# First cross attention: VectorE copies half of the last turned keys and takes the first maxima as keys arrive; the first scales of the last feed-forward are loaded in the SSM layer

## The reference, cut to what matters

```python
q, k, v = _fq_sym(q * scale, -1), _fq_sym(k, -1), _fq_sym(v, 2)   # round(x/s) clipped to +-127, times s
attn = softmax(einsum('bhqd,bhkd->bhqk', q, k))
attn = _fq_unsigned(attn, -1)                                      # s = row maximum / 255
x = x + einsum('bhqk,bhkd->bhqd', attn, v).reshape(B, N, C) @ Wp + bp
```

```python
vals = NVFP4_LUT[idx].reshape(N, K // 32, 32) * scales[:, :, None]    # gate, up, down
out = einsum('tn,hn->th', gelu_tanh(x @ Wg.T) * (x @ Wu.T), Wd)
```

## Time and profile before

| | us |
|---|---|
| median of three runs | 1578.74 |
| profiled execution, its own time | 1576.28 |
| its span | 1574.6 |
| TensorE busy | 1397.5 (89%) |
| VectorE busy | 1095.3 (70%) |
| ScalarE busy | 865.7 (55%) |
| GpSimd busy | 444.6 (28%) |
| mean granted clock of TensorE | 0.935 |

### The profile page before, as it was taken

The page is one execution under the profiler, slowest core; times in us unless marked ns, Lnnn a source line. Parts: engine busy times, 40 slices in busy tenths (PEclk is TensorE's granted clock), DMA queues, the critical chain, the costliest instruction groups (busy, mean ns, idle before and its releaser), DMA issues. The chain is left out here.

```text
span 1574.6 us, 23902 instructions
## 1 busy us (share of the span) xinstructions
PE 1397.5 (89%) x8036; PEld 981.6 (62%) x8036; DVE 1095.3 (70%) x2239; ACT 865.7 (55%) x2299; POOL 444.6 (28%) x515
## 2 busy tenths in 40 slices
PE   7876989866999689998679899999998989999969
PEld 5653444434776347876557678787877446666657
DVE  4687989834666566664568776765663779999953
ACT  2446989842123355425444545545454579999831
POOL 2244000000000000530346325533500047777710
PEclk9986999977999789998789999999999999999979
DMA  4001999975340322300200000000002344433120
GB/s 147 1 1 41 180 182 186 185 176 166 112 162 0 78 63 41 109 1 1 68 14 14 14 14 2 14 1 1 1 1 69 101 146 121 117 102 104 41 80 8
DMA packets 192390, 112.89 MB, mean 72 GB/s; under 512 B 150233, under 2 KB 166617, under 8 KB 191628
## 3 DMA queue, kind: packets, MB, share of 16 engines
q1 hardware_dynamic: 192268, 111.35, 27.6%
HBM read 77.51 MB, written 0.26 MB: 49 GB/s over the span
## 5 line engine op out<-in xcount | busy, mean ns | idle before, releaser
L671 DVE TENSOR_REDUCE x_row_max<-banks 128x1 f32<-128x512 f32 x248 | 152.6, 682 | 14.3 <-PE banks L365 13.9
L574 ACT ACTIVATE x_v_full<-banks,x_neg_max,x_q_scale 128x1024 int16<-128x1024 f32 x128 | 153.3, 1202 | 14.8 <-DMA x_v_full<-x_v_full 7.8
L211 PE MATMUL banks<-a_w_ring,x_normed_T 128*128 128x512 f32 x320 | 148.0, 603 | 4.8 <-DVE a_r L3189 4.8
L2670 DVE TENSOR_TENSOR ctx_tokens<-ctx_tokens,banks 128x512 f32<-128x512 f32 x128 | 87.8, 686 | 82.1 <-ACT x_weights_T L2556 60.2
L2388 PE MATMUL banks<-ctx_tokens,x_kT 128*128 128x512 f32 x272 | 140.1, 602 | 2.9 <-ACT ctx_tokens L2550 2.3
L2409 PEld LDWEIGHTS banks<-x_v,x_weights_T 128*128 128x128 f32 x896 | 113.0, 194 | 20.8 <-issue 17.6
L2409 PE MATMUL banks<-x_v,x_weights_T 128*128 128x129 f32 x896 | 118.1, 278 | 2.1 <-ACT x_weights_T L2566 2.1
L365 PE MATMUL banks<-x_kT_parts,x_qT_int 64*128 64x512 bf16 x512 | 105.2, 409 | 7.0 <-DVE x_row_max L671 3.3
L2504 POOL TENSOR_TENSOR ctx_tokens<-ctx_tokens 128x512 f32<-128x512 f32 (+1 forms) x48 | 65.8, 1372 | 141.7 <-DVE ctx_tokens L2650 141.7
L426 PEld LDWEIGHTS banks<-x_v_full,x_v_int 128*16 128x16 f16 x1024 | 57.5, 91 | 75.8 <-DMA x_v_full<-x_v_full 41.9
L211 PEld LDWEIGHTS banks<-a_w_ring,x_normed_T 128*128 128x128 f32 x320 | 59.6, 194 | 69.4 <-issue 69.4
(11 more groups left out here) (527 smaller groups left out, 3240.8 us busy)
## 6 DMA issues: line engine op xcount, KB each, us to landing
a_w_ring<-in_L_attn_WB_T SPq DMA_DIRECT2D x16, 512.0 KB
a_w_ring<-in_L_attn_WC_T SPq DMA_DIRECT2D x16, 512.0 KB
f_w_gate_up<-in_L_ffn_gate_up SPq DMA_DIRECT2D x18, 352.0 KB
ctx_tokens<-in_ctx SPq DMA_DIRECT2D x16, 256.0 KB, 5.8
x_wq<-in_L_xattn_Wq_T SPq DMA_DIRECT2D x8, 512.0 KB, 3.7
a_w_ring<-in_L_attn_Wth_T SPq DMA_DIRECT2D x8, 512.0 KB
a_bias_ring<-in_L_attn_B_bias_perm SPq DMA_DIRECT2D x16, 256.0 KB
a_bias_ring<-in_L_attn_C_bias_perm SPq DMA_DIRECT2D x16, 256.0 KB
```

The lines of the kernel that those rows point to most:

```text
L211: last = nc.tensor.matmul(out, lhsT, rhs, start=(i == 0), stop=(i == len(pairs) - 1))
L574: nc.scalar.activation(eb[:, q % RING], k.ps[:, 2 + 2 * (q % 2):4 + 2 * (q % 2), :].rearrange("p a n -> p (a n)"), ACT.Exp, bias=nb[:, v % ...
L671: nc.vector.reduce_max(mx[:, u % 2, i:i + 1], k.bank(MBANK[m % 3]), AX.X).then_inc(s.max_taken, 1)
L2670: nc.vector.tensor_tensor(flat(top), flat(top), bank, ALU.max).then_inc(s.maxed, 1)
```

## The change

In the first cross attention, for the last three pairs of keys (`ALONE` = 13 and up), ScalarE copies only the first block of a pair and VectorE the second, with a semaphore of its own, `kT_half_taken`. `kt_taken` is the wait for either. The maxima of tiles 4 to 7 move between these copies, on TensorE and on VectorE. GpSimd's casts of the values move one round later. ScalarE's wait for the cleared `ot` moves to its first write there.

In the other part a tile `first_scales` is allocated outside the layers. Its three loads are issued in the SSM layer, behind w_out; the feed-forward loads chunks 1 to 3 only and reads chunk 0 from the new tile.

```diff
+        ALONE = NP - 3
+        def kt_taken(engine, j, i):
+            if j < ALONE:
+                engine.wait_ge(s.kT_taken, 2 * j + i + 1)
+            elif i == 0:
+                engine.wait_ge(s.kT_taken, 2 * ALONE + j - ALONE + 1)
+            else:
+                engine.wait_ge(s.kT_half_taken, j - ALONE + 1)
...
                         if j >= 1:
-                            pe.wait_ge(s.kT_taken, 2 * (j - 1) + i + 1)
+                            kt_taken(pe, j - 1, i)
...
-                for i in range(4, 8):
-                    first_max(i)
+                    if j == NP:
+                        first_max(4)
+                        first_max(5)
+                    if j > NP:
+                        first_max(5 + j - NP)
...
-                    if NP // 2 + 4 <= j < NP // 2 + 8:
-                        g = j - NP // 2 - 4
+                    if NP // 2 + 5 <= j < NP // 2 + 9:
+                        g = j - NP // 2 - 5
...
                 def take_keys(j):
-                    for i in range(2):
+                    for i in range(1 if j >= ALONE else 2):
...
                 def take_output(v):
+                    if v == 0:
+                        act.wait_ge(s.zeroed, 2)
...
                 act.wait_ge(s.v_ready, 4)
-                act.wait_ge(s.zeroed, 2)
...
+                def take_half(j):
+                    dve.wait_ge(s.kT_in_psum, 2 * j + 2)
+                    a = (2 * j + 1) * P
+                    nc.vector.tensor_copy(kt[:, :, a:a + P], k.ps[:, 5, :].bitcast(BF16).rearrange("p (h n) -> p h n", n=P)).then_inc(s.kT_half_taken, 1)
+                for j in range(NP, NP + 3):
+                    take_half(j - 3)
+                    if j == NP:
+                        first_max(4)
+                        first_max(5)
+                    else:
+                        first_max(5 + j - NP)
```

```diff
@@ l3_attn, SyncE, behind the load of w_out
+                for j in range(len(MATS)):
+                    sp.dma_start(k.first_scales[:, j], A["L3_ffn_scales_T"][j, :, 0:CW].unsqueeze(1).to_broadcast([8, 16, CW])).then_inc(k.p_loaded[0], 16)
@@ l3_ffn
-                for c in range(NC):
+                for c in range(1, NC):
...
+                    by = k.first_scales[:, j] if c == 0 else scale[:, j, sl]
@@ build
+        k.first_scales = k.sb("f3_first_scales", [P, len(MATS), CW])
```

More of the change, by code:

```diff
@@ L273, in l0_xattn @@
         names = ("dve_step ctx_first x_loaded wq_loaded filled masks_ready bias_loaded bias_ready3 k_in_psum v_in_psum k_taken v_taken kf_ready hi_ready mid_ready "
[L274 removed]
+                 "rest_ready parts_ready kT_in_psum kT_taken kT_half_taken q_in_psum q_parts_ready qT_in_psum qT_taken xt_ready vmax_ready vmaxT_in_psum "
                  "vdiag_ready vscale_in_psum vscale_ready v_int_ready v_ready max_scores max_taken bias_ready exp_scores exp_done pT_used "
@@ L368, in first_max @@
                 def first_max(i):
-                    pe.wait_ge(s.kT_taken, 4 * (i + 1))
+                    for half in range(2):
+                        kt_taken(pe, 2 * i + 1, half)
                     if i >= 2:
@@ L506, in _ @@
                         nc.gpsimd.tensor_tensor(part(m, 2), kr[:, m % 2], part(m, 1), ALU.subtract).then_inc(s.parts_ready, 1)
-                    if NP // 2 + 4 <= j < NP // 2 + 8:
-                        g = j - NP // 2 - 4
+                    if NP // 2 + 5 <= j < NP // 2 + 9:
+                        g = j - NP // 2 - 5
                         pool.wait_ge(s.v_int_ready, g + 1)
                         nc.gpsimd.tensor_copy(vq[:, VG * g:VG * (g + 1)], vi[:, g]).then_inc(s.v_ready, 1)
-                pool.wait_ge(s.kT_taken, NKT)
+                kt_taken(pool, NP - 1, 0)
+                kt_taken(pool, NP - 1, 1)
                 nc.gpsimd.memset(ot[:], 0.0).then_inc(s.zeroed, 1)
@@ L3315, in weights @@
                     sl = slice(c * CW, (c + 1) * CW)
+                    by = k.first_scales[:, j] if c == 0 else scale[:, j, sl]
                     value = k.fp4[:, j, sl].bitcast(F8).rearrange("p (n v) -> p v n", v=2)
-                    nc.vector.scalar_tensor_tensor(out=wd[:, j, c % 2], in0=value, scalar=64.0, in1=scale[:, j, sl].unsqueeze(1).to_broadcast([P, 2, CW]),
+                    nc.vector.scalar_tensor_tensor(out=wd[:, j, c % 2], in0=value, scalar=64.0, in1=by.unsqueeze(1).to_broadcast([P, 2, CW]),
                                                    op0=ALU.mult, op1=ALU.mult).then_inc(s.w_ready, 1)
```

1 line of the change is left out of this document (removed).

## The result

| | before | after |
|---|---|---|
| median, us | 1578.74 (1577.45 to 1583.26, 5 runs) | 1565.41 (1563.71 to 1572.09, 5 runs) |
| profiled execution, its own time | 1576.28 | 1565.09 |
| its span | 1574.6 | 1563.3 |
| mean granted clock | 0.935 | 0.938 |

The changed kernel is faster: ratio 0.9918, 95% interval 0.9901 to 0.9936. A second measurement of the changed kernel (e14) gave 0.9930 (0.9916 to 0.9944).

A forecast was written before the change was run, and what follows sets the result against it. Bounds: waits for scales in the last feed-forward and for the memset and last keys in the first cross attention. Gains of 2.3 and 2.7 us, together 5.0, off 1578.74 gave 1573.7 us; range 1570.2 to 1577.3.

The forecast's parts named there:

- T2: Last feed-forward, scales loaded early: first product 4.67 us earlier, less 2.0 for a clock fall, 2.7 us gained.
- Rival 1: Last feed-forward: the clock holds through TensorE's gap, early scales give 4.7 us, total 1571.7 us; chance 0.25.
- T1: First cross attention: earlier memset release, shared key copies and moved casts together gain 2.3 us.
- T1b: First cross attention, last keys: VectorE takes three copies from ScalarE; 0.3 us gained, or 0.2 lost if copies are slow.
- T1a: First cross attention: ScalarE no longer waits for GpSimd's memset before its table load; 1.3 us gained.
- T1c: First cross attention: GpSimd's casts one round later no longer slow VectorE's product of keys; 0.7 us gained, bound 0.
- Rival 2: First attention gives nothing, as transposing DMAs bind the stage behind the exponentials; 1576.0 us; chance 0.15.
- rival 3: Last feed-forward: second scale group lands no earlier, first product stays, only the attention gain remains; 1576.4 us; chance 0.08.
- rival 4: Stage of exponentials: ScalarE runs ahead, waits for transposing DMAs grow, kernel slower, up to 1586.6 us; chance 0.06.

The follow-up runs named there:

- e14: Changed kernel itself, unchanged, measured a second time against the kernel before: ratio 0.9930 (0.9916 to 0.9944).
- e2: Kernel before with only the scales part (`first_scales`) of the change added: ratio 0.9951.
- e4: Kernel before itself, unchanged, measured and profiled once more: ratio 0.9991.
- e10: Kernel before with two more VectorE maximum operations behind the last addition of the first cross attention: second feed-forward 77.03 us.
- e11: Kernel before with one more VectorE maximum operation behind the last addition of the first cross attention: third self-attention 46.40 us.
- e16: Kernel before with one small VectorE maximum more, its result unread, behind the first cross attention: median 1574.70 us, ratio 0.9975.
- e17: Kernel before with one VectorE memset split in two in the third feed-forward, behind the layers in question: second feed-forward 79.62 us.
- e3: Kernel before with only ScalarE's wait for the cleared output tile moved to its first output: ratio 0.9988.
- e6: Changed kernel without the scales part and with GpSimd's casts in their old rounds: ratio 0.9967.
- e15: Kernel before with GpSimd's memset of the output tile split into two halves: 5 us slower (2 to 7).
- e8: Changed kernel with the second chunk's scales loaded behind the third's: last feed-forward 61.22 us.

## Why the prediction was wrong, point by point

Two steps failed: a fall of the clock that did not come, and the layers outside the diff, which the sum put at nothing. Of the 8.3 us between forecast and median, 2.0 stand against the first and some 3 against the second. Earlier loads are 0.75 us, the attention 0.2 to 0.5, and 2 us are left.

**T2, the clock's price: the first step that failed.** The forecast took 4.67 us of earlier product and subtracted 2.0 for a fall of the clock in a gap of 2.4 us. The product came 5.4 us earlier against its norm (11.10 instead of 16.52 us behind it): 4.67 and 0.75 for loads that landed sooner. That they landed sooner because nine stood in the queue and not twelve is not shown: in e2, also with nine, the same three landed 8.47 us behind the first issue, as the first three did before, and with twelve the first three landed anywhere from 7.6 to 8.6 us behind it. And the clock did not fall. T2 was 5.4 in place of 2.7, also alone (e2: 4.7). I had interpolated a threshold between a gap of 1.24 us that held and one of 2.9 that fell. The runs show gaps of 1.94, 2.05 and 2.72 that held and one of 2.09 that fell. The gap's length alone does not decide in that stretch, so from the rows of before neither outcome could be called the likelier. Rival 1 had 0.25 and came nearest, with 1571.7.

**T1, the attention: about right.** In x0 seven profiled kernels with the copies took 331.3 to 333.9 us, mean 332.4. Seven with neither the copies nor any edit of the waits (before, e2, e4, e10, e11, e16, e17), less what their added operations take, took 333.2 to 338.1, mean 335.2. That is 2.8 us for 2.3 forecast, with a scatter of 1 to 2 us between executions. Counted from the key product of round 13 to the first exponential, where most of the scatter is gone, it is 2.5 us (32.9 instead of 35.4 in the mean of the same kernels), and from there to the next layer both groups take the same (196.4 and 196.5 us, again less the added operations), as the forecast assumed. The parts were differently mixed. T1b was the largest, 1.7 us from e3 to e6: the copy takes 0.69 us, and TensorE turned the last pair at the higher clock. T1a was smaller, 0.8 us in e3, since the table load is now late for TensorE's scores. T1c was 0.2 to 0.3 us beside the copies: the small operation that waits beside the cast (1.65 us) takes back most of what the product gains. That is near its bound 0. That VectorE's copies do not wait for the casts beside them is borne out: the copies at 136.29 and 138.74 lie in the casts of 135.10 and 138.05 and take 0.69 us all the same.

**The untouched layers: the second step that failed.** The sum T1 + T2 puts every other layer at nothing and gives no reason for it. 2.5 us in f1 or a2 and some 0.5 in x2, f2 and x3 came with every kernel that has VectorE instructions added ahead of them, be it one or three. By their ratios e16, e10 and e11, less the operations' own 0.4, 2.5 and 1.2 us, give 4.3, 3.4 and 2.1 us; I take 3. The profile of before does not show which side of the clock's step a layer will come to lie on, so the size could not be forecast. But the layers behind the change have low-clock stretches, and the range had no room for such a step.

**The sum.** 5.4 + 2.8 + 3 = 11.2 us, beside 13.3 and 11.9 between the medians of the two measurements. The first interval reaches from 10 to 16 us, so the remaining 2 us are no sign of a further cause; an identical program showed -1.4 us (e4). That T1 came within 0.5 us of its forecast is in part luck: T1b was 1.4 us too low, T1a and T1c 0.5 us each too high.

**Rivals.** Rival 2 (attention gives nothing) falls with the exponentials, which start 2.5 us earlier and take no longer, and with e15, rival 3 with e2, and rival 4 with the waits, 13.1 us in 14 pieces as before.

What stays open is why one more VectorE instruction, or two or three, shortens the pauses. The rows show what it does: pauses of 0.30 instead of 0.58 us ahead of f1 and of 0.31 instead of 0.67 us in x2, with them an earlier start of f1 and a2 against the clock's fall, and by that a clock that rises 3.4 us earlier in one of the two. The last link rests on 17 executions that sort without an exception, closely in f1 (1.98 and 2.02 us); no run set the distance by itself. Where an instruction stands in memory is nothing that these traces show.

## What to carry to other kernels

Price a gap of the matmul engine with both outcomes of the clock and give each its own chance, unless a row of the same kernel has this gap behind as much work at the higher clock. Compare traces layer by layer, untouched layers too: a kernel with fast and slow clock stretches can gain or lose steps of microseconds where nothing was edited, and a control with one idle instruction tells such a step from the edit's own effect. Count the start of such a layer from the clock's last change, not from the kernel's start. Where executions scatter, measure an edit from the last instruction ahead of it. An operation that is off the path only by a little (the memset: 3.5 us longer, and the kernel was 5 us slower, 2 to 7) is worth a look at who waits for it.

## What the runs showed of the hardware that was not expected

- An added VectorE instruction of some tenths of a microsecond made the program 4 us faster (0.9975, 0.9963 to 0.9986), through layers 200 us and more further on, in one of which the clock rose earlier. Which layer it was went in 17 of 17 executions with the time from the layer's start to the fall of the clock; in f1 0.04 us lay between the two outcomes.
- Gaps of TensorE of 2.05 and 2.09 us in the same place of the same layer had different outcomes for the clock; the fall cost 1.7 us of time there (e6) and 2.25 us behind a gap of 7.26 us (e8).
- A VectorE copy of 128x1024 bf16 out of PSUM takes 0.69 us, as long as one of 128x512 f32. The Trainium skill (VectorE: DVE Perf Modes, section on why PSUM operands drop a tier) says that 16-bit copies from PSUM still go at two elements a cycle, and the trace agrees.
- A GpSimd memset of 64 partitions takes 3.50 us, as long as one of 128 partitions (3.51).
